# Mixer loop of four engines written out: VectorE, ScalarE, GpSimd and SyncE without a loop, order unchanged

## What is computed

```python
x = x + attn_a(layernorm(x), ...)   # scan over time, 8 heads, state 64 x 128
x = x + ffn(layernorm(x), W_r, W_k, W_v, mu_r, mu_k)
x = x + attn_b(layernorm(x), ...)   # short filter, then a long convolution
x = x + ffn(layernorm(x), W_r, W_k, W_v, mu_r, mu_k)

# attn_a, one step in time
h = alpha * h + beta * Bx_prev + gamma * Bx_t
y_t = einsum('bhpn,bhn->bhp', h, Cp_t)
# ffn
out = sigmoid(xr @ W_r) * (square(relu(xk @ W_k)) @ W_v)
```

## Time and profile before

| | |
|---|---|
| median of 3 runs | 4827.45 us (4822.77 to 4828.96) |
| profiled execution, its own time | 4829.95 us |
| its span, first to last instruction | 4828.2 us |
| mixer's rounds in the loop (4 to 29), as TensorE sees them | 676.53 to 3337.70 us of the span |
| TensorE busy | 4325.3 us, 90% |
| VectorE, ScalarE, GpSimd busy | 3193.5, 2149.7, 2345.0 us |
| fetches of instructions | 323 packets with 5.29 MB, 263 with 2.15 MB |

### The profile page before, as it was taken

The page is one execution under the profiler, slowest core; times in us unless marked ns, Lnnn a source line. Parts: engine busy times, 40 slices in busy tenths (PEclk is TensorE's granted clock), DMA queues, the critical chain, the costliest instruction groups (busy, mean ns, idle before and its releaser), DMA issues. The chain is left out here.

```text
span 4828.2 us, 121179 instructions
## 1 busy us (share of the span) xinstructions
PE 4325.3 (90%) x39924; PEld 3566.1 (74%) x39924; DVE 3193.5 (66%) x6762; ACT 2149.7 (45%) x5049; POOL 2345.0 (49%) x3277
## 2 busy tenths in 40 slices
PE   5259999999999999999989999999977999989999
PEld 3128777777777777777777777777756888878888
DVE  8456666666666666666666666666644666658888
ACT  3124444434444434444344444344435666655555
POOL 3026666556566656665656665566620000006666
PEclk9569999999999999999999999999988999999999
DMA  8120111111111111111111111111106666643333
GB/s 270 75 78 25 39 42 36 45 35 39 43 35 35 45 36 39 42 37 44 35 40 42 33 36 46 35 39 42 33 29 166 182 183 184 183 131 98 106 105 96
DMA packets 369510, 348.11 MB, mean 72 GB/s; under 512 B 24665, under 2 KB 342937, under 8 KB 359833
## 3 DMA queue, kind: packets, MB, share of 16 engines
q1 hardware_dynamic: 352028, 323.88, 22.6%
q10 hardware_dynamic: 16896, 16.78, 1.0%
HBM read 231.91 MB, written 108.66 MB: 71 GB/s over the span
## 5 line engine op out<-in xcount | busy, mean ns | idle before, releaser
L747 PE MATMUL bank<-w_bc,xnT 128*128 128x512 f32 x3072 | 815.3, 408 | 92.8 <-DVE rot L1189 52.4
L747 PEld LDWEIGHTS bank<-w_bc,xnT 128*128 128x128 f32 x3072 | 567.7, 191 | 238.2 <-issue 122.7
L950 ACT COPY turned_t<-bank 128x512 f32<-128x512 f32 x512 | 300.0, 586 | 947.8 <-PE bank L770 947.8
L1188 DVE TENSOR_TENSOR rot<-bank,par 128x512 f32<-128x512 f32 x512 | 352.2, 688 | 303.8 <-PE bank L747 177.9
L1483 PE MATMUL p_yc<-sig,toep 64*64 64x256 f32 (+14 forms) x16384 | 539.6, 282 | 14.5 <-issue 10.3
L1483 PEld LDWEIGHTS p_yc<-sig,toep 64*64 64x64 f32 x16384 | 476.2, 132 | 90.9 <-issue 44.2
L1077 POOL TENSOR_TENSOR steps<-upto,par 128x512 fp32r<-128x512 f32 x512 | 537.3, 1069 | 0.0
L1086 POOL TENSOR_TENSOR turned_b<-rot 128x512 f32<-128x512 f32 x256 | 325.6, 1272 | 179.6 <-DVE rot L1189 179.6
L1069 POOL TENSOR_TENSOR xnT<-xnT_raw,xnT 128x256 fp32r<-128x256 f32 x128 | 94.5, 739 | 605.8 <-ACT xnT L929 605.8
L1189 DVE TENSOR_TENSOR rot<-bank,par 128x512 f32<-128x512 f32 x512 | 348.0, 680 | 0.0
L1632 POOL MEMSET xT<- 128x258 f32 x1 | 0.3, 314 | 687.1 <-POOLq L1377 687.1
(11 more groups left out here) (259 smaller groups left out, 9701.4 us busy)
## 6 DMA issues: line engine op xcount, KB each, us to landing
toep<-taps_dram SPq DMA_DIRECT2D x256, 260.0 KB, 4.2
el<-el_dram SPq DMA_DIRECT2D x256, 128.0 KB, 3.0
xg<-arg_x SPq DMA_DIRECT2D x32, 512.0 KB, 4.7
xnT_dram<-xt_g ACTq DMA_DIRECT2D x32, 512.0 KB, 4.0
xnT_raw<-xnT_dram SPq DMA_DIRECT2D x128, 128.0 KB, 2.9
x_quad<-arg_x SPq DMA_DIRECT2D x32, 512.0 KB, 4.2
x_dram<-x_quad SPq DMA_DIRECT2D x32, 512.0 KB, 3.2
x0T_dram<-conv SPq DMA_DIRECT2D x32, 512.0 KB, 2.8
```

The lines of the kernel that those rows point to most:

```text
L747: last = mm(p_bc[c][:, :], xnT[w.q % 2][p][:, k, :], w_bc[q][:, k, c * 1024 + g * W4:c * 1024 + (g + 1) * W4], start=(n == 0), stop=(n == ...
L950: s_.copy(turned_t[g][c][:, :], p_tr[:, :]).then_inc(s[f"copy_{BC[c]}"], 1)
L1188: v_.tensor_tensor(heads(rot1[c][:, :]), heads(p_bc[c][:, :]), cos, ALU.mult)
```

## The change

The four loops are gone. `rounds` no longer has a loop for any engine: it takes `body` alone and calls it for `n` from 0 to 33 with Python integers. The number of a round is a constant everywhere, and steps outside 0 to 127 (tiles) or 0 to 31 (quads) are left out as before. Two increments of a semaphore `pool_go` on GpSimd, on which nothing waited, are dropped, and the semaphore with them. TensorE's program is the same.

```diff
-    PEELED, AHEAD = 4, 2
     Place = namedtuple("Place", "n q p")
-    def rounds(eng, body, unrolled=False):
-        def one(n, u):
-            known = isinstance(n, int)
+    def rounds(body):
+        for n in range(QUADS + 2):
             def tile(q, lag, step, *args):
-                if not known or 0 <= QUAD * n + q - lag < TILES:
-                    step(QUAD * n + (q - lag), Place(n + (q - lag) // QUAD, (q - lag) % QUAD, (u + (q - lag) // QUAD) % 2), *args)
+                i = QUAD * n + q - lag
+                if 0 <= i < TILES:
+                    step(i, Place(i // QUAD, i % QUAD, i // QUAD % 2), *args)
             def quad(lag, step, *args):
-                if not known or 0 <= n - lag < QUADS:
-                    step(n - lag, (u - lag) % 2, *args)
+                if 0 <= n - lag < QUADS:
+                    step(n - lag, (n - lag) % 2, *args)
             body(tile, quad, n)
-        if unrolled:
-            for n in range(QUADS + 2):
-                one(n, n % 2)
-            return
-        for n in range(PEELED):
-            one(n, n % 2)
-        with eng.Fori(PEELED // 2, (QUADS - AHEAD) // 2) as g:
-            for u in range(2):
-                one(2 * g + u, u)
-        for n in range(QUADS - AHEAD, QUADS + 2):
-            one(n, n % 2)
...
-            rounds(sp, body)
+            rounds(body)
...
-                pool.sem_inc(s["pool_go"], 1)
```

More of the change, by code:

```diff
@@ L581, in mixer_and_first_ffn @@
              "residual1 rstd1 norm1 xn_over first_column shifted mixed key relu key_sq receptance tanh value gated residual2 rstd2 norm2 "
-             "x2n_over x2_hi x2_lo widen took taps halo short_filter setup pool_go load_xnT0 load_xnT1 load_par0 load_par1 load_x0 load_x1 load_el0 load_el1 "
+             "x2n_over x2_hi x2_lo widen took taps halo short_filter setup load_xnT0 load_xnT1 load_par0 load_par1 load_x0 load_x1 load_el0 load_el1 "
              "store_x2 store_x0 store_vx").split()
@@ L917, in body @@
                     tile(q, 0, decay_logs, 1)
-            rounds(pe, body, unrolled=True)
+            rounds(body)
         @block.scalar
@@ L1054, in body @@
                         quad(1, normalised, 2, 0)
-            rounds(act, body)
+            rounds(body)
         @block.gpsimd
@@ L1173, in body @@
                         quad(1, layer_rstd, 2, 0)
-            rounds(pool, body)
+            rounds(body)
         @block.vector
@@ L1333, in body @@
                         quad(1, residual2, 0)
-            rounds(dve, body)
+            rounds(body)
 def long_convolution(nc, ctx, t):
```

## The result

The changed kernel takes 4799.13 us (median of five, 4794.9 to 4800.31), the kernel before 4828.64 us in the same comparison. The ratio is 0.994, 95% interval 0.9925 to 0.9954: 29.5 us or 0.6% faster. The forecast was 4796.3 us and 31.1 us less.

A forecast was written before the change was run, and what follows sets the result against it. TensorE, busy 90% of the span, was taken as the bound, waiting in the transitions. Jumps and clock gave 31.1 us (15.8 us of it sure), entry/exit, register arithmetic, DMA issue and program length zero: 4827.45 - 31.1 = 4796.3 us, range 4776 to 4816.

## What to carry to other kernels

A hardware loop whose jump stands where all engines hand over to one another costs each pass its refetch on the engine with the least slack; price it by comparing rounds with and without a jump, not by the longest pause or the named wait. If the program can't be written out, more work per pass gives most of it (five jumps instead of twelve gave 22.1 us, none gave 29.5); moving the jump to a place where ScalarE had slack and VectorE had none gave nothing, and a place where every looping engine has slack was not tried. And look at what the pause was hiding: the same in-order wait that made the jump expensive was worth 69 us when it was moved.

## What the runs showed of the hardware

- In the kernel before, the sequencer's next instruction starts 2.8 to 3.1 us after a taken jump on VectorE, 2.5 to 2.9 on ScalarE and 2.5 to 2.6 on GpSimd, but 0.3 us on SyncE, while the branch instruction itself takes 40 to 72 ns. The engine stands less where its sequencer had run ahead: ScalarE some 1.9 us. With VectorE alone in the loop, each of its pauses holds an 8 KB instruction fetch.
- Straight code is not free either: in rounds 4 to 29 of the changed kernel VectorE pauses 0.4 to 0.5 us in 20 places, which are multiples of 128 instructions apart. No fetch is under way in these pauses; one starts 0.65 to 1.15 us after each.
- The same transition, with 4.2 us of idle time in each case, takes 17.8 us at a mean granted clock of 0.90 and 18.8 or 19.2 at 0.82 (rounds 9, 8 and 6 of the changed kernel). The mean clock tells the short from the long, not the two long ones from each other. A disturbance of 2 us in one round can lengthen the next, undisturbed one by 0.9 us on the mean (19.44 against 18.53).
